# A fused attention and mixture-of-experts layer on one core: the last chunk's shared expert put behind the expert tiles, and the steps of the last head group placed anew

## What is computed

```python
def layer(x):                                   # x: (1, 2048, 256)
    x = x + attention(layernorm(x))
    return x + ffn(layernorm(x))

def attention(x):                               # weights rounded to three levels per group of 128
    q, k, v = split(ternary_linear(x, w_qkv))   # 16 query heads, 4 key/value heads, 16 features each
    q, k = rotary(rms_norm(q)) * q_gain, rotary(rms_norm(k))
    y = softmax(causal(q @ k.T / 4)) @ v
    return ternary_linear(rms_norm(y), w_proj)

def ffn(x):
    score = sigmoid(x @ w_router)               # 8 experts, the best 2 for each token
    out = sum(weight[e] * (silu(x @ w1[e]) * (x @ w3[e])) @ w2[e] for e in top2(score))
    return out + (silu(x @ ws1) * (x @ ws3)) @ ws2      # the shared expert, 352 hidden columns
```

## Time and profile before

| | |
|---|---|
| runs | 561.7 us median of 3 (556.29 to 564.91) |
| the profiled execution | 561.11 us, of which its span 559.3 us |
| busy in the span | PE 478.0 us, ACT 356.4, DVE 312.1, POOL 184.7 |
| mean granted TensorE clock | 0.923 |

### The profile page before, as it was taken

The page is one execution under the profiler, slowest core; times in us unless marked ns, Lnnn a source line. Parts: engine busy times, 40 slices in busy tenths (PEclk is TensorE's granted clock), DMA queues, the critical chain, the costliest instruction groups (busy, mean ns, idle before and its releaser), DMA issues.

```text
span 559.3 us, 9883 instructions
## 1 busy us (share of the span) xinstructions
PE 478.0 (85%) x3202; PEld 268.6 (48%) x3202; DVE 312.1 (56%) x881; ACT 356.4 (64%) x557; POOL 184.7 (33%) x244
## 2 busy tenths in 40 slices
PE   1586999999899996999998987968978799999970
PEld 1573333333233331333343532436867699998960
DVE  6976354745732146522166374376876266666637
ACT  3246798989799994999879466553341245555520
POOL 3722102025852227550310143052155024444420
PEclk9988799999899997999999778888979889999995
DMA  8121107154961479504479021046113324444359
GB/s 217 25 56 43 44 15 229 32 117 97 263 187 48 110 196 298 169 6 110 112 253 419 33 76 40 8 123 153 38 58 106 95 76 124 124 117 131 96 164 334
DMA packets 61243, 69.09 MB, mean 124 GB/s; under 512 B 12259, under 2 KB 53443, under 8 KB 60579
## 3 DMA queue, kind: packets, MB, share of 16 engines
q1 hardware_dynamic: 57499, 58.74, 37.3%
q0 software_dynamic: 3408, 9.34, 4.7%
q10 hardware_dynamic: 288, 0.39, 0.3%
HBM read 32.68 MB, written 26.22 MB: 105 GB/s over the span
## 4 chain that ended last, share of the span: by engine, by line
PE 54%; DVE 18%; issue 8%; ACT 8%; DMA 6%; SPq 4%; POOL 1%; another core or an unknown queue 1%; ACTq 0%; DVEq 0%; POOLq 0%
PE ps L1599 16%; PE ps L1579 11%; PE ps L1781 7%; ACT prob L815 7%; PE ps L1800 3%; PE ps L1726 2%; PE ps L1519 2%; PE ps L1635 2%; PE ps L1772 2%; PE ps L1804 2%; PE ps L1608 2%; PE ps L1649 2%; PE ps L1790 2%; PE ps L1540 2%; DVE y_sb L1465 1%
## 5 line engine op out<-in xcount | busy, mean ns | idle before, releaser
L815 ACT ACTIVATE prob<-ps 128x1024 f32<-128x1024 f32 (+3 forms) x320 | 259.8, 924 | 53.9 <-PE ps L1579 52.4
L1599 PE MATMUL ps<-prob,v_sb 128*32 128x512 f32 (+3 forms) x1280 | 158.2, 569 | 7.1 <-POOL prob L659 6.0
L1579 PE MATMUL ps<-qk 64*128 64x512 f32 (+3 forms) x640 | 121.3, 443 | 10.5 <-ACT prob L815 6.9
L659 POOL TENSOR_SCALAR_AFFINE_SELECT prob<-prob 128x512 f32<-128x512 f32 x64 | 42.2, 662 | 206.5 <-ACT prob L815 206.2
L1579 PEld LDWEIGHTS ps<-qk 64*128 64x128 f32 x640 | 54.1, 192 | 106.8 <-ACT prob L815 87.0
L751 POOL DMA_INDIRECT pair_out<-yo,xg x39 | 37.8, 970 | 65.4 <-DVE yo L1445 65.1
L1599 PEld LDWEIGHTS ps<-prob,v_sb 128*32 128x32 f32 x1280 | 25.9, 110 | 53.4 <-issue 33.9
L1726 PE MATMUL ps<-x2T,ws 128*128 128x512 f32 (+1 forms) x144 | 41.7, 444 | 0.9 <-DVE hid L1322 0.9
L1103 DVE COPY o_sb<-ps 128x512 f32<-128x512 f32 x16 | 11.1, 691 | 51.9 <-PE ps L1599 51.6
L712 POOL DMA_INDIRECT rows_by_expert<-xs,slots x32 | 31.3, 978 | 19.1 <-DVE slots L1286 10.4
L1726 PEld LDWEIGHTS ps<-x2T,ws 128*128 128x128 f32 (+1 forms) x144 | 29.2, 210 | 9.3 <-DVE hid L1322 1.4
(11 more groups left out here) (193 smaller groups left out, 706.0 us busy)
## 6 DMA issues: line engine op xcount, KB each, us to landing
qk<-qT SPq DMA_DIRECT2D x138, 64.0 KB, 2.1
w_parts<-parts SPq DMA_DIRECT2D x16, 352.0 KB
w<-w_parts SPq DMA_DIRECT2D x2, 2816.0 KB, 14.4
xg<-rows_by_expert SPq DMA_DIRECT2D x39, 129.0 KB
yfin<-pair_out SPq DMA_DIRECT2D x8, 512.0 KB, 7.3
raw<-in_w SPq DMA_DIRECT2D x8, 352.0 KB
w_parts_d<-parts SPq DMA_DIRECT2D x16, 176.0 KB
w_parts<-w_parts_d SPq DMA_DIRECT2D x1, 2816.0 KB
```

Of the source, the lines that this page charges most:

```text
L659: nc.gpsimd.affine_select(out=t, in_=t, compare_op=ALU.is_ge, fill=0.0, base=0, pattern=[[0, HPG], [1, P]], channel_multiplier=-1).then_in ...
L815: nc.scalar.activation(prob[:, u % NPB, 2 * hf:2 * hf + 2, c0:CH], ps[:, b:b + 2, c0:CH], ACT.Exp, scale=SCALE).then_inc(exp_done, 1)
L1579: ins = M(ps[:, 2 * (n % NSB) + h, c0:CH], qk[rows, par, PAIRS, kt * P:(kt + 1) * P], qk[rows, par, hf, j * CH + c0:(j + 1) * CH], start=T ...
L1599: ins = M(ps[VW * h:VW * (h + 1), O_BANK, c0:CH], v_sb[:, kt, :], prob[:, u % NPB, h, c0:CH], start=(kt == 0), stop=(u == LAST_OF[j]), ski ...
```

## The change

1. `rsqrt` has ten linked instructions in place of twelve: another first guess, one step of four instructions that corrects by a quadratic, and one Newton round.
2. In the middle groups norm_qk is cut in squares_qk (before output(g,1)) and scale_qk (behind it).
3. SPLIT_AT: group 1 takes 3, 5 and 3 pieces (was 2, 4, 3), group 2 takes 5 and 3 (was 2, 5, 3). SP handles eight pieces before the moves for group 2 (was six).
4. LAST_GROUP and AFTER are new; step (4, 2) goes from the last group to AFTER. AFTER is called behind the first half of up, the second half, and down.
5. Of the 16 high parts, seven stay on ACT and nine are made by DVE (`both_parts`), eight of these inside the last group.
6. `choose` is cut in `choose` and `weigh`; DVE's order in and behind the last group is new; scale_x2(0) now stands before output(g,1); `ends` is published in place(3).
7. ACT writes three of the eight padding blocks (`pad_rows`), SP the other five.
8. Low parts of items 0, 4, 6, 9, 10 and 11 are DVE's, the others POOL's (was: POOL 0 to 3). On POOL those of 7 and 8 stand behind the sends of chunk 3.
9. Items 9, 10 and 11 all come behind the tiles (was: 11 alone), with finish(0) between hidden_low(10) and hidden(11) on DVE.

```diff
-    1: [("out", 1, 3)], 4: [("out", 0, 0)], 5: [("step", 0, 0)], 6: [("step", 1, 0)], 8: [("step", 2, 0)],
-    9: [("step", 3, 0)], 12: [("out", 0, 1)], 14: [("step", 4, 0)], 15: [("step", 5, 0)], 16: [("step", 0, 1)],
-    17: [("step", 1, 1)], 18: [("step", 6, 0)], 19: [("step", 2, 1)], 20: [("step", 3, 1)], 22: [("step", 7, 0)],
-    24: [("out", 0, 2)], 26: [("step", 4, 1)], 27: [("step", 5, 1)], 28: [("step", 0, 2)], 29: [("step", 1, 2)],
-    30: [("step", 6, 1)], 31: [("step", 2, 2)], 32: [("step", 3, 2)], 34: [("step", 7, 1)], 39: [("step", 4, 2)],
+    0: [("out", 1, 3)], 4: [("out", 0, 0)], 5: [("step", 0, 0)], 6: [("step", 1, 0)], 8: [("step", 2, 0)],
+    9: [("step", 3, 0)], 12: [("out", 0, 1)], 13: [("step", 4, 0)], 16: [("step", 5, 0)], 17: [("step", 6, 0)],
+    18: [("step", 0, 1)], 20: [("step", 1, 1)], 22: [("step", 2, 1)], 23: [("step", 7, 0)], 24: [("out", 0, 2)],
+    25: [("step", 3, 1)], 26: [("step", 0, 2)], 29: [("step", 1, 2)], 31: [("step", 4, 1)], 32: [("step", 5, 1)],
+    33: [("step", 6, 1)], 34: [("step", 2, 2)], 36: [("step", 3, 2)], 37: [("step", 7, 1)],
...
-    (0, 0): [("out", 0, 3), ("step", 5, 2)], (1, 0): [("step", 0, 3), ("step", 1, 3), ("step", 6, 2)],
-    (2, 0): [("step", 2, 3), ("step", 3, 3)], (4, 0): [("step", 4, 3), ("step", 5, 3)],
-    (5, 0): [("step", 7, 2), ("step", 6, 3)], (6, 1): [("step", 7, 3)],
+    (2, 0): [("out", 0, 3), ("step", 4, 2)], (2, 1): [("step", 5, 2)], (2, 2): [("step", 6, 2), ("step", 0, 3)],
+    (3, 0): [("step", 1, 3)], (3, 2): [("step", 2, 3), ("step", 3, 3)], (4, 0): [("step", 7, 2)],
+    (5, 1): [("step", 4, 3), ("step", 5, 3)], (5, 2): [("step", 6, 3)], (6, 2): [("step", 7, 3)],
...
-SPLIT_AT = {(1, 3): 2, (1, 11): 4, (1, 23): 3, (2, 3): 2, (2, 11): 5, (2, 23): 3}
+SPLIT_AT = {(1, 3): 3, (1, 11): 5, (1, 23): 3, (2, 11): 5, (2, 23): 3}
+HIGH_ON_ACT = (("step", 1, 0), ("step", 0, 2), ("step", 4, 2), ("step", 5, 2), ("step", 1, 3), ("step", 4, 3),
+               ("step", 5, 3))
...
-            next_pieces(0, 6)
+            next_pieces(0, 8)
             for c in range(NC):
                 move(2, c)
-            next_pieces(6, 9)
+            next_pieces(8, 11)
...
-            for e in range(E):
+            for e in range(PADS_BY_ACT, E):
                 end = nc.sync.value_load(ends[0:1, e:e + 1], min_val=e * SEG, max_val=e * SEG + T)
                 sp.dma_start(rows_d[bass.ds(end, P), :], pads_d[e * P:(e + 1) * P, :]).then_inc(padded, 16)
...
+            hidden_low(1)
+            hidden_low(2)
+            hidden_low(3)
             send_rows(2, 0)
             send_rows(2, 1)
+            hidden_low(5)
             send_rows(3, 0)
             send_rows(3, 1)
+            hidden_low(7)
+            hidden_low(8)
...
+            def pad_rows():
+                act.wait_ge(ends_ready, 1)
+                act.wait_ge(padded, 32)
+                for e in range(PADS_BY_ACT):
+                    end = nc.scalar.value_load(ends[0:1, e:e + 1], min_val=e * SEG, max_val=e * SEG + T)
+                    nc.scalar.dma_start(rows_d[bass.ds(end, P), :], pads_d[e * P:(e + 1) * P, :]).then_inc(padded_act, 16)
...
-                for _ in range(3):
-                    link(V.tensor_tensor(t, y, y, ALU.mult))
-                    link(V.scalar_tensor_tensor(t, t, -0.5, a, ALU.mult, ALU.mult))
-                    link(V.scalar_tensor_tensor(y, t, 1.5, y, ALU.add, ALU.mult))
+                link(V.tensor_tensor(t, y, y, ALU.mult))
+                link(V.scalar_tensor_tensor(t, t, 64.0 / 9.0, a, ALU.mult, ALU.mult))
+                link(V.scalar_tensor_tensor(t, t, -10.0 / 3.0, t, ALU.add, ALU.mult))
+                link(V.scalar_tensor_tensor(y, t, 5.0, y, ALU.add, ALU.mult))
+                link(V.tensor_tensor(t, y, y, ALU.mult))
+                link(V.scalar_tensor_tensor(t, t, -0.5, a, ALU.mult, ALU.mult))
+                link(V.scalar_tensor_tensor(y, t, 1.5, y, ALU.add, ALU.mult))
...
                 output(g, 0)
-                norm_qk(g + 1, 0, NT)
+                squares_qk(g + 1, 0, NT)
                 output(g, 1)
+                scale_qk(g + 1, 0, NT)
                 rotate(0, NT)
...
+                if ("step", n, j) in HIGH_ON_ACT:
+                    dve.wait_ge(high_ready, HIGH_ON_ACT.index(("step", n, j)) + 1)
                 else:
-                    dve.wait_ge(x2T_hi_ready, 2 * j + n - 3)
-                    hi, lo = x2T_hi[j][:, n - 4, :], x2T_lo[j][:, n - 4, :]
+                    link(V.tensor_copy(hi, ps[:, bank, :]))
                 V.tensor_tensor(lo, ps[:, bank, :], hi.bitcast(F32), ALU.subtract).then_inc(x_free, 1)
...
             row_stats(0, LN)
+            scale_x2(0)
             output(g, 1)
-            scale_x2(0)
             row_stats(1, RMS)
...
+            for n in range(FLAT_FIRST, FLAT - 1):
+                hidden(n)
+                hidden_low(n)
+            finish(0)
             hidden(FLAT - 1)
             hidden_low(FLAT - 1)
-            finish(0)
             finish(1)
             take_shared(NC - 1)
```

More of the change, by code:

```diff
@@ L836, in exp_logits @@
                 nc.scalar.activation(sc[:, 1], sc[:, 0], ACT.Exp, scale=-1.0).then_inc(score_ready, 1)
-            def steps(events):
-                for kind, *args in events:
-                    if kind == "step" and args[0] in (0, 1, 4, 5):
-                        high_part(*args)
             for u in range(NU):
@@ L918, in _ @@
                     tile_out_low(i - 2)
-            silu(FLAT - 1)
-            hidden_high(FLAT - 1)
+            for n in range(FLAT_FIRST, FLAT):
+                silu(n)
+                hidden_high(n)
         @block.vector
@@ L1349, in _ @@
             row_stats(0, LN)
+            scale_x2(0)
             output(g, 1)
[L1351 removed]
             row_stats(1, RMS)
[L1353 to L1355 removed]
             rms_scale(1)
[L1357 removed]
+            both_parts(4, 0)
+            both_parts(5, 0)
             logits(0)
+            choose(0)
+            both_parts(0, 1)
+            weigh(0)
+            both_parts(1, 1)
             add_residual(2, 1)
+            copy_output(g, 2)
@@ L1373, in _ @@
+            both_parts(4, 1)
+            both_parts(5, 1)
             logits(1)
+            choose(1)
             add_residual(2, 2)
+            weigh(1)
             add_residual(3, 2)
-            choose(1)
-            place(1)
             row_stats(2, LN)
             scale_x2(2)
-            low_part(4, 2)
             copy_output(g, 3)
+            hidden(0)
+            place(1)
+            hidden(1)
+            hidden_low(0)
             take_output(g, 3)
-            low_part(5, 2)
@@ L1385, in _ @@
             row_stats(3, RMS)
-            hidden(0)
-            low_part(0, 3)
-            low_part(1, 3)
+            both_parts(4, 2)
+            both_parts(5, 2)
             rms_scale(3)
             logits(2)
-            hidden(1)
+            hidden(2)
+            both_parts(0, 3)
+            choose(2)
+            both_parts(1, 3)
+            hidden(3)
+            weigh(2)
             add_residual(2, 3)
             add_residual(3, 3)
-            hidden(2)
             row_stats(3, LN)
@@ L1396, in _ @@
             scale_x2(3)
-            choose(2)
-            hidden(3)
-            low_part(4, 3)
-            low_part(5, 3)
+            place(2)
+            take_shared(0)
+            both_parts(4, 3)
+            both_parts(5, 3)
             hidden(4)
-            place(2)
+            hidden(5)
+            hidden_low(4)
             logits(3)
-            hidden_low(4)
-            take_shared(0)
-            hidden(5)
             choose(3)
-            hidden_low(5)
+            weigh(3)
@@ L1409, in _ @@
+            place(3)
+            list_tiles()
             hidden(6)
-            place(3)
+            hidden(7)
+            take_shared(1)
             hidden_low(6)
-            hidden(7)
-            list_tiles()
-            take_shared(1)
-            hidden_low(7)
             hidden(8)
-            hidden_low(8)
-            hidden(9)
-            hidden_low(9)
-            hidden(10)
-            hidden_low(10)
             assert X_LAST + len(ORDER) == xuse["base"] + xuse["n"]
@@ L1760, in _ @@
             pe.wait_ge(ld_ws, 48)
-            for n in range(FLAT - 1):
-                up(n)
-                after((n, 0))
+            for n in range(FLAT_FIRST):
+                for w in range(2):
+                    up(n, w)
+                    after((n, w))
                 if n >= 2:
                     down(n - 2)
-                after((n, 1))
+                    after((n, 2))
+            down(FLAT_FIRST - 2)
+            down(FLAT_FIRST - 1)
             assert xuse["n"] == len(ORDER)
```

159 lines of the change are left out of this document (86 added, 73 removed).

## The result

The changed kernel takes 542.8 us in the median of 4 runs (540.7 to 543.0), beside 562.7 for the kernel before (556.3 to 564.9); the ratio is 0.969, interval 0.964 to 0.974. It is faster, and 542.8 lies inside the range of 519 to 545, but the gain is 19.9 us where 30.3 were forecast. The profiled run took 542.99 us.

What follows compares the result with a forecast made beforehand. The middle groups run at PE's pace; the last group is loose, its waits also lowering PE's clock. Terms -1.2 - 2.5 - 6.2 - 11.2 - 5.6 - 5.3 + 1.7 = -30.3 from 561.11 gave 531 us, range 519 to 545.

Steps and rivals of the forecast that it cites:

- Roots: Preamble: each root loses two links of 0.20 us, three roots lie on the chain that ended last; -1.2 us.
- Head norm: Group 1: DVE's copy of O_BANK comes earlier, waits -1.1 us and lower clock -1.4; -2.5 us.
- Pieces: Group 2: without a piece at (2, 3), PE's 4.75 us mask wait and 1.4 of clock go; -6.2 us.
- "I take 0" for group 1: Group 1: the burst at unit 11 grows by about one load wait, counted as 0; other bound some 3 us.
- if the wait for pieces returns in group 1: Group 1: one of the signs named beforehand by which the prediction would be wrong; no size given.
- Last group: Last group: 88.4 us against 99.57, waits going, a new 3.1 us wait for o_sb included; -11.2, bounds -16 and -3.
- Attention's end to slots: From attention's end to chunk 3's slots: 47.2 us against 52.86; -5.6 us, bounds -9 and -2.
- 1.5 for waits that I did not see: Attention's end to slots: allowance of 1.5 us for unseen waits, within the 47.2 us.
- Padding: Slots to first tile: five pads at 1.67 us each and earlier `ends` gain 6.2, sends up to 0.9 late; -5.3 us.
- Tail: Behind the tiles: finish(1) starts at 549.1 instead of 547.42, the rest follows as now; +1.7 us.
- Items 9 and 10 in front: Before the tiles: leaving out items 9 and 10 frees only PE time that waited for xg anyway; 0 us.
- Rival one: Last group and next stage: new waits replace old ones, gains only 3 and 2 us, time 542.6; chance 0.20.

Runs made afterwards that it cites:

- after_again: The changed kernel, unchanged, timed and profiled once more in another set: 527.6 us, ratio 0.961 to the kernel before.
- the two pairs: Two pairs of profiles of the kernel before and the changed kernel, the second under another condition: span changes -18.1 and -21.4 us.
- pads_0: The changed kernel with all eight padding blocks issued by SP, none by ACT: 540.1 us, ratio 0.967 to the kernel before.
- experiment 7: Only the copy of o_sb moved ahead of scale_x2(0), against the changed kernel with group 1 pieces 3, 4, 4: 533.1 us against 535.8.
- before_again: The kernel before, unchanged, run once more for its profile: 547.4 us.
- experiment 8: Items 9 and 10 put ahead of the tiles again, on the changed kernel with group 1 pieces 3, 4, 4; two versions: 528.4 and 526.2 us.
- items_before_2: Items 9 and 10 ahead of the tiles, hidden(11) before finish(0), on the changed kernel with group 1 pieces 3, 4, 4: 526.2 us against 524.8.

## Why the prediction missed 12 us, by its steps

The step that failed outright is in group 1, the pieces taken at 0; more than half of the missing time is there. The three stages before the tiles were walked as lengths of 88.4, 47.2 and 16.9 us. The profile of the result has 90.1, 49.5 and 18.8, but after_again has 85.6, 46.4 and 15.2, none longer than the walk. In the first two of these stages the gain falls short there only because the kernel before is shorter as well.

**Roots, -1.2:** -0.7 and -1.6 in the two pairs. The same preamble took 2.8 us less in pads_0 than in the changed kernel, so these agree with the forecast and don't prove it.

**Head norm, -2.5:** right in kind, about -2 with the pieces out of the way.

**Pieces, -6.2 in group 2:** right (-6.6). **"I take 0" for group 1: wrong, and the costliest step.** It cost 6.1 to 6.5 us in the profile of the result (75.70 against 69.6 and 69.2), and 2.8 in after_again. I had given the burst one wait for a load more. In fact the loads feed the burst at their own pace: five pieces from 144.49 to 161.76, 3.5 us each, where POOL's work on one is 2.5. My bound of 3 us came from the one late load of the earlier trace rows; the row that I should have used is the time between two landings, times the pieces in the burst beyond those already loaded. The test I had named, "if the wait for pieces returns in group 1", is what came.

**Last group, -11.2:** -9.5. The 3.1 us for o_sb came as worked out (3.05), and experiment 7 shows that with its clock it cost 3.3 to 3.6, and could have been avoided. Among the waits that go I had put 2.7 us for x2's low part. That one wasn't the order's to win: in the kernel before it follows a remote wait of ACT's high part,

```profile
341.04 0.59 ACT L827 CAST x2T<-ps 128x512 fp32r<-128x512 f32 x1 [3.92 <-remote]
```

and before_again has neither; there ACT waits 1.16 us for PE in its place. The changed kernel gets a stall of the same kind under ACT L824, and PE waits 3.87 us for it at 335.65. In the pair without stalls the group gains 6.9.

**Attention's end to slots, -5.6:** -3.4 and -2.8. The two waits I had found came (1.4 and 1.1 us forecast, 1.51 and 0.66 measured). "1.5 for waits that I did not see" was too little here: the stage is 2.3 us longer than the 47.2 of the walk, and DVE alone stands 4.30 us at L1279 and 2.33 at L1317,

```profile
376.70 0.22 DVE L1279 TENSOR_REDUCE sc<-ps 128x32 f32<-128x64 f32 x1 [4.30 <-remote]
...
406.65 0.19 DVE L1317 TENSOR_TENSOR sc<-ps,reach 128x32 f32<-128x32 f32 x1 [2.33 <-remote]
```

and in after_again, without them, two small instructions of DVE near there last longer than elsewhere (0.18 and 0.23 us):

```profile
365.00 2.58 DVE L1287 TENSOR_SCALAR sc<-sc 128x32 f32<-128x32 f32 x1
...
392.37 1.67 DVE L1318 TENSOR_TENSOR picked<-choice,sc 128x64 f32<-128x64 f32 x1
```

The stage is 3.1 us shorter there, 46.4, and so within 0.8 us of the walk. The gain is missed even so, since the kernel before is 3.7 us shorter in this stage too: the 52.86 us from which the walk was subtracted held time that no order of steps had to win. What it was in the kernel before I can't name; its profile has no remote wait in that stage.

**Padding, -5.3:** -3.4 and -6.1, of the latter 3.8 up to the issue of xg. The 1.67 us a pad was the mis-sized term: five took 2.55 each in one condition and 1.15 in the other. In the condition without the slow stretch five pads end at 401.6, POOL's last send is issued at 404.26, and the sends set the hand-over, as the sum had it.

**Tail, +1.7:** +1.5 as walked (+0.5 in the second pair, where the tail of the kernel before is 0.9 us longer). **Items 9 and 10 in front, 0:** wrong without stalls. There they delay the first tile by 3.4 us (experiment 8), and 2.3 of the 6.1 us of the second pair are theirs. PE's wait for xg covered them only in the profile that I had read, with 2.99 us of it left; without stalls it doesn't: in items_before_2 the first transposes, at 411.45, have no such wait left.

Rival one, new waits for old ones, gave 542.6 and the median is 542.8. That is luck: its two stages were to gain 3 and 2 us and gained 9.5 and 3.4, and the pieces took most of the difference back. The lower end of the range, 519, doesn't follow from the terms given for it: -16, -9 and no delay by POOL make 521.7.

## To carry over

When work that waits for transfers is moved into a burst, price the burst by the interval at which transfers land, not by one late transfer. Before a chain is put ahead of a copy that TensorE needs, ask whether the copy alone can go first: 0.7 us ahead of some 3.3 us of roots and scaling left 0.65 us of a wait of 3.06. A duration that is a mean over a row of issues (13.37 us for 8) may hide two rates; look at the single ones before multiplying. And before an idle stretch is booked as a gain, it is worth a second profile of the kernel before, to see whether the stretch is the kernel's.

## What was not expected of the hardware

In one condition, waits whose end the profile ascribes to nobody stand at the same instructions in all eight profiles of the changed kernel and its variants: DVE L1279 4.2 to 4.3 us, L1317 2.3, ACT L877 4.0 to 4.6. Others come in some of the eight only, up to 5.9 us (ACT L869 in pads_0). In the other condition there is none, but DVE L1287, or the same line moved, takes 2.5 to 2.6 us in all seven profiles, 14 times its usual 0.18.

Is it an engine that waits for its own code? I had thought so, as the DMA view of the changed kernel for 374 to 377 us, where L1279's wait ends, has one packet of the queue for instructions:

```profile
q8 instruction: 1, 0.02, 2.9%
```

The traces don't bear it out. The view for 374 to 376.5 us has no such packet and that for 376.5 to 378 has it, so it starts only as the wait ends, at 376.70. And the view for 399.5 to 428 us, with the waits before L1317 and L877 that end at 406.6, has no instruction packet at all. The cause stays open. The condition moved the kernel before by 9 to 14 us (from 548.8 and 550.6 to between 559.6 and 562.7) and the changed one by 15 (527.6 to 542.8), more than most of the edits here.
